# One value slot in the key product, value copies on two engines, and three moves in the step order of a windowed-attention kernel

## What is computed

```python
xn = _layernorm(xt, norm1_g, norm1_b)            # per token, 48 channels
xw = windows_7x7(roll(xn, -3))                   # 16 x 16 windows of 49 tokens
q, k, v = split(xw @ qkv_w + qkv_b)              # 3 heads of 16
attn = softmax(q @ k.T * dh ** -0.5 + bias)      # 49 x 49 per window and head
out = (attn @ v) @ proj_w + proj_b
x = x + roll(unwindow(out), 3)
h = gelu(_layernorm(x, norm2_g, norm2_b) @ fc1_w + fc1_b)
x = x + h @ fc2_w + fc2_b
```

## Time and profile before

| | |
|---|---|
| median of three executions | 1960.83 us |
| profiled execution, device time | 1975.34 us |
| its span on the core | 1973.7 us |
| PE busy over the span | 1772.9 us (90%) |
| ACT busy | 1541.7 us (78%) |
| DVE busy | 1365.0 us (69%) |
| POOL busy | 1170.0 us (59%) |
| mean granted clock of TensorE | 0.951 of full speed |

### The profile page before, as it was taken

The page is one execution under the profiler, slowest core; times in us unless marked ns, Lnnn a source line. Parts: engine busy times, 40 slices in busy tenths (PEclk is TensorE's granted clock), DMA queues, the critical chain, the costliest instruction groups (busy, mean ns, idle before and its releaser), DMA issues. The chain is left out here.

```text
span 1973.7 us, 90330 instructions
## 1 busy us (share of the span) xinstructions
PE 1772.9 (90%) x38186; PEld 1076.4 (55%) x38186; DVE 1365.0 (69%) x2016; ACT 1541.7 (78%) x2904; POOL 1170.0 (59%) x1048
## 2 busy tenths in 40 slices
PE   4999999999999999999999998995899967999996
PEld 2666556656565565655666565651497943333332
DVE  7776666767676676766767676642777766888883
ACT  3788788888888788888888888873766647888882
POOL 5687686777778677777877777652255550122222
PEclk9999999999999899999999999996799985999998
DMA  4344554444444344444444444411488759999994
GB/s 111 94 108 99 139 129 103 105 102 110 100 113 102 96 107 100 116 99 105 106 107 103 104 112 99 98 45 43 109 216 216 214 135 170 227 253 253 262 258 147
DMA packets 233228, 262.26 MB, mean 133 GB/s; under 512 B 167079, under 2 KB 179911, under 8 KB 232711
## 3 DMA queue, kind: packets, MB, share of 16 engines
q1 hardware_dynamic: 217478, 217.50, 46.2%
q0 software_dynamic: 15360, 39.08, 6.6%
HBM read 160.82 MB, written 80.88 MB: 122 GB/s over the span
## 5 line engine op out<-in xcount | busy, mean ns | idle before, releaser
L416 POOL TENSOR_TENSOR shift<-const_b,qmax 113x588 bf16<-113x588 bf16 x256 | 299.4, 1170 | 231.8 <-DVE qmax L511 230.1
L563 DVE TENSOR_TENSOR x<-ps_m,x 112x392 f32<-112x392 f32 x128 | 66.5, 561 | 272.8 <-PE ps_m L1028 272.8
L511 DVE TENSOR_REDUCE qmax<-ps_s 113x12 f32<-113x588 f32 x256 | 194.9, 761 | 66.8 <-PE ps_s L907 66.7
L1487 POOL DMA_DIRECT2D out_rolled<-r_OUT x128 | 63.8, 503 | 270.2 <-DVE r_OUT L1587 270.2
L716 ACT ACTIVATE P<-ps_t 113x588 f32<-113x588 f32 x256 | 172.0, 672 | 58.4 <-PE ps_t L959 57.1
L748 ACT ACTIVATE G<-ps_m 128x392 f32<-128x392 f32 x384 | 178.3, 500 | 46.0 <-PE ps_m L1009 45.5
L503 DVE TENSOR_TENSOR Ul<-Uf 113x784 bf16<-113x784 f32 x192 | 208.5, 1113 | 0.0
L1333 PE MATMUL conv_ps<-xin,band_now 64*64 64x448 bf16 x2688 | 203.1, 364 | 2.2 <-DVE x_low L1228 2.2
L406 POOL TENSOR_TENSOR xhl<-xh 113x784 bf16<-113x784 f32 x64 | 200.7, 3137 | 2.2 <-DVE xh L551 2.2
L709 ACT COPY Uf<-ps_m 113x392 f32<-113x392 f32 x384 | 172.9, 486 | 33.0 <-PE ps_m L874 24.8
L1333 PE MATMUL conv_ps<-x_low,band_now 64*64 64x448 bf16 x1344 | 179.6, 351 | 0.0
(11 more groups left out here) (244 smaller groups left out, 5203.9 us busy)
## 6 DMA issues: line engine op xcount, KB each, us to landing
xin<-rows_scratch SPq DMA_DIRECT2D x96, 236.0 KB, 3.8
XT<-x_tokens SPq DMA_DIRECT2D x64, 294.0 KB, 3.3
X<-x_windows SPq DMA_DIRECT2D x128, 147.0 KB, 3.4
RS<-rs_scratch SPq DMA_DIRECT2D x128, 147.0 KB, 3.4
XR<-x_windows SPq DMA_DIRECT2D x128, 147.0 KB, 3.2
x_scratch<-x SPq DMA_DIRECT2D x128, 147.0 KB, 3.4
y_scratch<-y POOLq DMA_DIRECT2D x96, 196.0 KB, 2.9
r_RS<-rs_scratch SPq DMA_DIRECT2D x128, 147.0 KB, 4.6
```

The source lines that it names most:

```text
L416: nc.gpsimd.tensor_tensor(shift[:, j % 2], e, m, ALU.mult).then_inc(S["md"], 1)
L511: nc.vector.tensor_reduce(qmax[:, j % 2, :].rearrange("p (b n) -> p b n", b=2), ps_s[0:R, :, 0:2 * HQ].rearrange("p b (n t) -> p b n t", t ...
```

## The change

1. `UV` becomes `HEADS` + 1: one value slot of 48 channels, without gaps. KVj's products are 196 columns wide instead of 245; their number stays. `wv_swap` goes, and the constants and `V` are laid out anew (`V[R, 2, QP, C, 2]`: channel, then upper or lower half, so that a window's own values and zeros alternate). The projection's two products now go by kind of window pair (`a`) with two weight layouts instead of by column half with one. Their number and width stay.
2. The copies of the values are made in two instructions of 49 partitions x 192 columns for each quad instead of one of 113 x 384. Quads 0, 2 and 3 are copied by DVE (six instructions per strip), quad 1 by ACT (two). `exp_scores` of quads 2 and 3 now waits for DVE's copy of the same quad, and DVE's copy of quad 0 waits for `exp_scores(s, 0)`.
3. On DVE, `u_low` of heads 1 and 2 moves behind `subtract_mean`, `divide(s, 1)` and the maxima.
4. On ACT, `square(prv)` moves behind the last gelu. On POOL, `low0(nx2)` and `squares_low(prv)` change places.
5. Setup: ACT spreads the values in 2 copies instead of 8, POOL makes low parts of half the width, and clears the larger `V`.

```diff
-        UV = HEADS + 2
+        UV = HEADS + 1
...
+        def kept(q):
+            return (S["vev"], 2 * (q // 4 * 3 + (0, 1, 1, 2)[q % 4])), (S["vev_mid"], 2 * (q // 4 + (q % 4 > 1)))
+
+        def kept_values(p, j):
+            lo = ROWB * p
+            to = V[lo:lo + TOK, j % 2, :, :, p].rearrange("p (b k) c -> p b k c", b=2)
+            of = ps_t[lo:lo + TOK, :, 0:2 * SV].rearrange("p b (k c) -> p b k c", c=SV)[:, :, :, HQ:HQ + C]
+            return to, of
...
 (POOL step)
-                squares_low(prv)
                 low0(nx2)
+                squares_low(prv)
...
+            def keep_values(s, j):
+                if s.real:
+                    q = 4 * s.n + j
+                    wait(dve, S["st"], q + 1)
+                    if j == 0:
+                        wait(dve, S["ex"], q + 1)
+                    wait(dve, S["pv"], q - 1)
+                    for p in range(2):
+                        nc.vector.tensor_copy(*kept_values(p, j)).then_inc(S["vev"], 1)
...
 (DVE step)
                 query_max(s, 2)
+                keep_values(s, 0)
                 token_sums(s.at(4))
...
                 divide(s, 0)
+                keep_values(s, 2)
                 u_low(nxt, 0)
-                u_low(nxt, 1)
                 subtract_mean(prv)
-                u_low(nxt, 2)
                 query_max(nxt, 0)
                 divide(s, 1)
+                keep_values(s, 3)
+                u_low(nxt, 1)
                 query_max(nxt, 1)
+                u_low(nxt, 2)
...
 (exp_scores)
+                    if j >= QUADS // 2:
+                        wait(act, *kept(q + 1)[0])
...
 (ACT step)
-                keep_values(s, 0)
...
-                keep_values(s, 2)
...
                 gelu(old, 0, 0)
-                square(prv)
                 gelu(old, 0, 1)
                 gelu(old, 1, 0)
-                keep_values(s, 3)
                 gelu(old, 1, 1)
                 gelu(old, 2, 0)
                 gelu(old, 2, 1)
+                square(prv)
```

More of the change, by code:

```diff
@@ L380, in _ @@
             nc.gpsimd.memset(eps_t[:], EPS0).then_inc(eps_made, 1)
-            for t in (wv, wv_swap, blank, margin, x2):
+            for t in (wv, V, blank, margin, x2):
                 nc.gpsimd.memset(t[:], 0.0).then_inc(cleared, 1)
@@ L452, in step @@
                 make_shift(nxt, 0)
+                low0(nx2)
                 squares_low(prv)
-                low0(nx2)
             for raw in range(-4, -1):
@@ L530, in first_residual @@
                     wait(dve, S["x2_made"], 2 * (s.n - 1))
-                    for b in range(2):
-                        wait(dve, S["proj"], 2 * s.n + b + 1)
+                    for a in range(2):
+                        wait(dve, S["proj"], 2 * s.n + a + 1)
                         nc.vector.scalar_tensor_tensor(
-                            out=x1[:, r, cols_of(b)], in0=bank("proj", b)[0:R, 0:HALF], scalar=out_b[:, 0:1],
-                            in1=XR[:, r, cols_of(b)], op0=ALU.add, op1=ALU.add).then_inc(S["x1_made"], 1)
+                            out=of_kind(x1[:, r, :], a), in0=bank("proj", a)[0:R, 0:HALF].rearrange("p (j t) -> p j t", j=QUADS),
+                            scalar=out_b[:, 0:1], in1=of_kind(XR[:, r, :], a), op0=ALU.add, op1=ALU.add
+                            ).then_inc(S["x1_made"], 1)
             def subtract_mean(s):
@@ L634, in _ @@
                 lo = ROWB * g
[L635 to L638, removed]
+                link(nc.vector.tensor_copy(wv[lo:lo + C + 1, 0:C], ps_s[lo:lo + C + 1, 1, 0:C]))
             assert chain[0] == WV_V
@@ L724, in keep_values @@
                     wait(act, S["pv"], q - 1)
-                    nc.scalar.copy(V[:, j % 2].rearrange("p (b n) c -> p b n c", b=2),
-                                   ps_t[0:R, :, 0:2 * SV].rearrange("p b (n c) -> p b n c", c=SV)[:, :, :, HQ:HQ + 2 * C]
-                                   ).then_inc(S["vev"], 1)
+                    for p in range(2):
+                        nc.scalar.copy(*kept_values(p, j)).then_inc(S["vev_mid"], 1)
             def invert_sums(s, j):
@@ L797, in _ @@
             for r in range(2):
-                for a in range(2):
-                    for n, t in enumerate((wv, wv_swap)):
-                        nc.scalar.copy(
-                            Uf[:, r, HEADS + a, cols_of(n)].rearrange("p (w t) -> p w t", t=TOK),
-                            t[:, TOK * a:TOK * a + TOK].unsqueeze(1).to_broadcast([R, WINS // 2, TOK])
-                        ).then_inc(values_spread, 1)
+                nc.scalar.copy(Uf[:, r, HEADS, :].rearrange("p (w t) -> p w t", t=TOK),
+                               wv[:].unsqueeze(1).to_broadcast([R, WINS, TOK])).then_inc(values_spread, 1)
             steps(step, -1, N + 2)
@@ L922, in keys_and_values @@
                     wait(pe, S["ex"], q)
-                    wait(pe, S["vev"], q)
+                    for copied in kept(q):
+                        wait(pe, *copied)
                     r = s.slot(2)
@@ L984, in project @@
                     wait(pe, S["nrm"], 4 * s.n + 4)
-                    for b in range(2):
-                        free_m("proj", b)
-                        mm(bank("proj", b)[0:R, 0:HALF], proj_w[:], O[:, s.slot(2), cols_of(b)],
+                    for a in range(2):
+                        free_m("proj", a)
+                        mm(bank("proj", a)[0:R, 0:HALF], proj_w[:, a, :], O[:, s.slot(2), a],
                            start=True, stop=True).then_inc(S["proj"], 1)
-                        taken("proj", b, S["x1_made"], 2 * s.n + b + 1)
+                        taken("proj", a, S["x1_made"], 2 * s.n + a + 1)
             def fc1(s, k):
@@ L1794, in constants @@
         ones[lo:lo + TOK, lo:lo + TOK] = 1
-        for b in range(2):
-            key_ones[lo:lo + TOK, b, DH * (g ^ b):DH * (g ^ b) + DH] = 1
+        key_ones[lo:lo + TOK, :, g] = 1
     out["picks"] = np.concatenate([pick, ones, minus], 1)
-    out["key_ones"] = key_ones.reshape(R, 4 * DH)
+    out["key_ones"] = key_ones.reshape(R, 2 * DH)
     out["eye"] = np.eye(128, dtype=f)
@@ L1859, in packs_of @@
         put(a, PACK_A, "w2_part", prm0["fc2_w"][F1:HID], F2 * g)
-        for h in range(HEADS):
-            put(a, PACK_A, "proj_w", prm0["proj_w"][DH * h:DH * h + DH], 2 * DH * h + DH * g, lo)
+        for kind in range(2):
+            first = PACK_A["proj_w"].start + R * kind + ROWB * (g ^ kind)
+            a[g:2 * C:2, first:first + C] = prm0["proj_w"]
         put(a, PACK_A, "bias", by_query, lo)
```

42 lines of the change are left out of this document (23 added, 19 removed).

## The result

The changed kernel takes **2016.76 us** (median of 4 runs, 2012.64 to 2018.53) where the kernel before, on the same chip, takes 1962.38 us (4 runs, the three named ahead of the prediction and one more). The ratio is 1.0264, with an interval of 1.0226 to 1.0301: 2.6% slower. The forecast was 1975, with a range to 1992. The profiled execution after is 2018.53 us (span 2016.9), 43.2 us above that of before.

The account below looks back on a forecast made before the run. PE, busy 540.5 of 580 us in attention, was taken to set the pace. +0.44 - 0.18 = +0.26 us per step, times 62 = +16, less 2 at setup, +14: 1975 us, own range 1965 to 1988, with rivals 1936 to 1992.

Parts of the forecast that it names:

- The key product: KV groups on PE: 0.092 us each instead of 0.115, 0.55 us per step of PE's work, of which only quad 3's counts.
- the 0.14 us: Quad 3 of the key product: its shorter groups lie on the path and save this much per step.
- the 0.04: Quad 3's exponential on ACT: comes earlier by at most 0.04 us, as quad 2's ACT copy ahead of it is gone.
- The value copies: Copies moved from ACT to DVE: about 1.6 us per step more on DVE, which does not become the bound.
- The gate: DVE's `divide(prv, 3)` ahead of the projection: projection at 814.28 instead of 814.25, so quads 0 and 1 gain nothing.
- The low parts: POOL's `low1` beside DVE's `Ul`: shrinks from 3.26 us to about 2.3 to 2.5.
- the two shifts: Ahead of fc1 0: `first_residual` 0.4 us later and a shorter `low1` cancel, leaving about nothing.
- Rival D: DVE and POOL become the gate: `low1` late and unshrunk, fc1 0 0.41 later, +0.59 per step more, 2012 us; chance 0.10.
- The square: ACT behind the last gelu: the path from first gelu to KV0 grows by 0.43 to 0.44 us per step.
- Setup: Before the first KV0: POOL's 8.01 us halve; between 0 and 4 us reach KV0, taken as 2 saved.
- The sum per step: Whole attention step: +0.44 for the square less 0.18 for quad 3, +0.26 us, times 62 = +16 us.

Follow-up runs that it names:

- a2: The changed kernel with the one low part still ahead of the mean moved behind it too; 1998.47 us, ratio to before 1.0138.
- a1: The changed kernel with the square back at its old place, behind the first gelu; 1989.01 us, ratio to before 1.0095.
- b1: The kernel before with one edit, the square moved behind the last gelu; 1998.57 us, ratio to before 1.0138.
- b2: The kernel before with one edit, the low parts of heads 1 and 2 moved behind the mean; 1968.37 us, ratio to before 0.9991.
- a4: The changed kernel with POOL's `low1` made on 16 of 784 columns only; 2009.25 us, one run.
- a5: The changed kernel with `low1` on 16 of 784 columns and POOL's token centring moved behind the next shift; 2115.98 us, one run.
- a6: The changed kernel with POOL's token centring moved behind the next shift and `low1` whole; 2142.72 us, one run.
- e1: The kernel before with one value slot, 196-column products and their setup; copies in pairs on ACT, engine orders as before; 1978.1 us, ratio 1.0047.

## Why the prediction was wrong

- *The key product.* Right. 0.09 us per group. The projection comes 5.34 us behind KV0 (816.68), as forecast, gated by the division (`[0.21 <-DVE O L546]`); `weigh(s, 1)` 10.12 behind it, before 10.09. Quads 0 to 2 gained nothing. Of quad 3, the 0.14 us came, the 0.04 didn't: KV3 is 11.76 behind KV0 as before.
- *The value copies.* The gate was right, by two errors that cancel. A pair takes 0.74 us, not 0.62, since the second does not overlap the first (355 ns each). In return `t_mean` takes 0.17 us instead of 0.49, so the token operations take 1.82 us instead of 2.11. That the projection came where it was forecast is thus luck. The load of DVE was worked out too low as well: six copies at the prediction's own 0.62 us a pair are 1.86 us per step and not 1.6, and they took 2.13 (136.5 us in 64 steps). The same 0.74 us stand ahead of `Ul` at quad 2, and there I had only asked whether quad 3 gets its exponential in time, not what is queued behind.
- *The low parts.* **This is the step that failed**: "the two shifts cancel and leave about nothing". I took from the earlier trace rows that `low1` is long because DVE is busy, and shrinks with the `Ul` that go. I did not ask which of the two engines has the turn and what happens to the one `Ul` that stays. It takes 1.72 us instead of 0.96, behind a copy pair of 0.74. So the mean is late, and fc1 0 with it. fc1 0 was to come 0.18 us sooner behind KV0 and it came 0.19 later (13.31 instead of 13.12): 0.37 us per step. With that low part behind the mean (a2) fc1 0 comes at 12.89. Rival D had the place and nearly the time (2012), but not the mechanism: `low1` did shrink, and fc1 0 waited for the mean. That its time is so near is luck: its sum was 0.85 us per step, and 0.69 came.
- *The square.* Right in kind, 0.06 us too small: KV0 follows the exponential by 0.10 us, not 0.05, and 6.65 us behind the first gelu instead of 6.59. a1 and b1 show it from both sides.
- *Setup.* The first KV0 came 2.3 us sooner, as forecast. But the sum took 62 whole steps and nothing for the fill, in which the moved low parts gate KV0 three times: 5.1 us later at the first load instead of 2 sooner, 7 us. b2, with that edit alone, shows the same (+6.3), and b1 doesn't (+0.1).

The sum per step was +0.26; with 0.37 and 0.06 it is +0.69, and 0.68 was measured in a regular step. Over the 63 distances that is 43 us, where 16 had been worked out; the fill adds 5, and the steps that are not regular, the long ones and the short last ones, give 5 back. Against the medians, the profiled execution of before lay 13 us above its median and that of after only 2, so that the 43 us of the profiles stand as 54 in the medians. The range had taken low and high from the forecast's own terms; none of them held a slower `Ul`.

## What to carry to other kernels

Where two engines block each other as DVE and POOL do here, ask of each pair of instructions which begins first, and what then stands behind the loser. An edit that takes work from one of them can hand the turn to the other, and busy time is no measure of it: POOL's `low1` gained 105 us here and the kernel lost 43. Before work is moved to the end of an engine's step, look at the first steps too, in which that end is what the next step waits for.

## What the runs showed of the hardware

- A two-input DVE instruction (`Ul`, 784 columns) takes 0.96 us alone. When a two-input POOL instruction is under way as it starts, it ends 0.82 to 0.84 us after POOL's end, in seven kernels (changed, before's third, a2, a4, a5, a6, b2), however long that is. The other way round `low1` ended 1.36 us after the second `Ul`, near its 1.49 alone. By the Trainium skill, page "GPSIMD Engine Reference", section "Specifications", POOL shares its SBUF interfaces with DVE and meets contention where DVE reads two SBUF inputs. The traces agree. In these rows the contention takes the form that whole instructions take turns, and the wait is part of the loser's record.
- DVE can be kept out through four POOL instructions in a row, 5.32 us (a5, a6). In other orders it gets in after one. I can't say what decides it.
- The start of a record is not when the work was served: before, POOL's `low1` has its start at 818.75 and DVE's `Ul` at 818.81, and it was DVE that went first. The traces of b2 show where it turns: from 100 to 1340 us `Ul` went first (0.96 us long) in all 119 cases in which POOL's record began 0.05 to 0.11 us ahead of it, and POOL in all 42 in which it began 0.13 or 0.14 ahead.
- Which of several waiting instructions comes next hangs on less than 0.1 us too: in e1 `low1` got in between two `Ul` in the 50 steps in which its record began 0.07 us or more behind the first, and had to wait for both in the 11 in which it began earlier.
- A small operation pays too: `t_mean` with 14 columns took 0.49 us before, beside a POOL shift that ended at 812.49, and 0.17 us after, with no POOL work beside it.
